# Probabilities times V: one matmul for each head in 32 array columns, and a plain copy of its output

## The reference

```python
q = (x @ Wq.T).reshape(B, N, H, d).transpose(0, 2, 1, 3)
kv = (y @ Wkv.T).reshape(B, N2, 2, H, d).transpose(2, 0, 3, 1, 4)
attn = jnp.einsum('bhnd,bhmd->bhnm', q * scale, k)
attn = jnp.where(pad_mask[:, None, :, None], attn, jnp.float32(-1000000000.0))
attn = jax.nn.softmax(attn, axis=-1)
out = jnp.einsum('bhnm,bhmd->bhnd', attn, v)
```

## Time and profile before

| what | value |
|---|---|
| median of three runs | 1987.46 us |
| the profiled execution's own time | 1987.12 us |
| its span, first to last instruction | 1985.3 us |
| granted TensorE clock, mean | 0.989 of 2.4 GHz |
| TensorE matmuls busy | 1889.8 us, 95% of the span |
| weight loads busy | 1466.3 us |
| VectorE busy | 1247.6 us |
| ScalarE busy | 1069.4 us |

### The profile page before, as it was taken

One profiled execution on the slowest core, in us unless ns is written; L12 is line 12 of the kernel. 1 busy time (PEld: TensorE's weight loads), 2 busy tenths in 40 slices (PEclk: granted clock), 3 DMA queues, 4 the chain that ended last, 5 costly groups with the idle time before them and its releaser, 6 DMA issues. The chain is left out here.

```text
span 1985.3 us, 39511 instructions
## 1 busy us (share of the span) xinstructions
PE 1889.8 (95%) x13922; PEld 1466.3 (74%) x13923; DVE 1247.6 (63%) x2287; ACT 1069.4 (54%) x1695; POOL 619.5 (31%) x641
## 2 busy tenths in 40 slices
PE   6999999999999999999999999999948999999997
PEld 6888888888888887888888888888734444444443
DVE  3555555554545555555555565555549999999995
ACT  3444444444444443434444444444318999999996
POOL 1101011010101111010101021010028999999994
PEclk9999999999999999999999999999979999999999
DMA  4111111111211111111221111111132222222221
GB/s 143 32 61 48 43 48 43 48 46 52 83 44 48 43 48 44 49 43 50 54 75 50 43 48 43 48 43 43 30 122 70 96 86 89 95 95 93 83 72 38
DMA packets 56198, 120.61 MB, mean 61 GB/s; under 512 B 5692, under 2 KB 5692, under 8 KB 56028
## 3 DMA queue, kind: packets, MB, share of 16 engines
q1 hardware_dynamic: 55828, 119.82, 18.8%
q10 hardware_dynamic: 328, 0.25, 0.0%
HBM read 101.64 MB, written 29.43 MB: 66 GB/s over the span
## 5 line engine op out<-in xcount | busy, mean ns | idle before, releaser
L417 ACT ACTIVATE prob<-psum,nmax 114x750 f32<-114x750 f32 x256 | 225.4, 885 | 251.7 <-DVE nmax L591 251.7
L338 POOL TENSOR_TENSOR y_l<-y,y_h 128x750 fp32r<-128x750 f32 x93 | 156.6, 1706 | 551.2 <-ACT y_h L403 551.2
L408 ACT ACTIVATE k_h<-psum 128x376 fp32r<-128x376 f32 (+1 forms) x256 | 124.0, 484 | 353.6 <-PE psum L846 352.2
L596 DVE TENSOR_TENSOR k_l<-psum,k_h 128x376 fp32r<-128x376 f32 (+1 forms) x256 | 139.7, 546 | 276.7 <-ACT k_h L408 276.0
L591 DVE TENSOR_REDUCE nmax<-psum 114x1 f32<-114x750 f32 x256 | 228.4, 934 | 104.2 <-PE psum L835 100.0
L846 PE MATMUL psum<-y_h,wkv_h 128*128 128x376 f32 (+1 forms) x768 | 277.1, 361 | 1.1 <-DVE q_l L584 1.1
L846 PE MATMUL psum<-y_l,wkv_h 128*128 128x376 f32 (+1 forms) x768 | 255.9, 333 | 0.0
L846 PE MATMUL psum<-y_h,wkv_l 128*128 128x376 f32 (+1 forms) x768 | 255.8, 333 | 0.0
L856 PE MATMUL psum<-wkv_h,y_h 128*125 128x512 f32 x576 | 237.6, 413 | 0.7 <-DVE wkv_l L655 0.7
L1441 PE MATMUL psum<-w_q,hq_t 128*128 128x512 bf16 x896 | 205.8, 383 | 25.4 <-ACT yo L1297 25.4
L856 PE MATMUL psum<-wkv_l,y_h 128*125 128x512 f32 x576 | 227.6, 395 | 0.0
(11 more groups left out here) (117 smaller groups left out, 3369.0 us busy)
## 6 DMA issues: line engine op xcount, KB each, us to landing
y<-in_ctx_t SPq DMA_DIRECT2D x32, 1125.0 KB, 8.0
w_part<-in_w_t SPq DMA_DIRECT2D x32, 512.0 KB, 8.1
xb<-in_x SPq DMA_DIRECT2D x56, 256.0 KB, 2.7
ab<-attn_rows SPq DMA_DIRECT2D x56, 256.0 KB, 2.9
out_rows<-yo SPq DMA_DIRECT2D x56, 256.0 KB, 2.0
attn_rows<-vmean_rows SPq DMA_DIRECT2D x32, 336.0 KB
attn_rows<-attn SPq DMA_DIRECT2D x32, 112.0 KB
xa<-in_x SPq DMA_DIRECT2D x30, 112.0 KB
```

The lines of the kernel that those rows point to most:

```text
L338: pool.tensor_tensor(y_l[:, slot, c, :], y[:, c, :], y_h[:, slot, c, :].bitcast(F32), ALU.subtract).then_inc(a_yl, 1)
L408: act.activation(k_h[:, g, s0:s1], ps_proj[k_bank[par][g, hf]][:, 0:s1 - s0], ACT.Copy).then_inc(a_kh, 1)
L417: act.activation(prob[:, e, :], ps_score[e][0:RP], ACT.Exp, bias=nmax[:, i:i + 1], accum_out=den[:, i:i + 1]).then_inc(p.exp, 1)
L596: dve.tensor_tensor(k_l[:, g, s0:s1], ps_proj[k_bank[par][g, hf]][:, 0:s1 - s0], k_h[:, g, s0:s1].bitcast(F32), ALU.subtract).then_inc(a_k ...
```

## The change

`weighted` takes each head by itself: 32 columns of V, the 57 columns of `prob_t` that belong to the head, and 32 output partitions of `ps_o`, which shrinks from [128, 4, 114] to [128, 4, 57]. So there are four matmuls for each chunk of keys where there were two, each half as wide in both directions, in four strips of 32 array columns. `heads_out` becomes one copy of 128 x 57. `head_one`, its eight memsets and the semaphore `own_o` go.

```diff
@@ set-up of tiles
-        head_col, head_one = sb("head_col", [128, 2]), sb("head_one", [128, 2])
+        head_col = sb("head_col", [128, 2])
-        ps_o = psum[:, 6, 0:NG * RP].rearrange("p (g n) -> p g n", g=NG)
+        ps_o = psum[:, 6, 0:NG * RM].rearrange("p (g n) -> p g n", g=NG)
@@ VectorE, set-up
                     for e in range(2):
                         dve.memset(head_col[HD * i:HD * i + HD, e:e + 1], SCALE if i % 2 == e else 0.0).then_inc(a_head, 1)
-                        dve.memset(head_one[HD * i:HD * i + HD, e:e + 1], 1.0 if i % 2 == e else 0.0).then_inc(a_head, 1)
-                dve.wait_ge(a_head, 4 * HPG)
+                dve.wait_ge(a_head, 2 * HPG)
@@ VectorE
                 def heads_out(p, n, g):
                     dve.wait_ge(p.o, NG * n + g + 1 + ONE)
-                    dve.tensor_scalar(o_t[:, g, :], ps_o[:, g, 0:RM], head_one[:, 0:1], 1.0, ALU.mult, ALU.mult).then_inc(own_o, 1)
-                    dve.wait_ge(own_o, 1)
-                    dve.scalar_tensor_tensor(out=o_t[:, g, :], in0=ps_o[:, g, RM:RP], scalar=head_one[:, 1:2], in1=o_t[:, g, :],
-                                             op0=ALU.mult, op1=ALU.add).then_inc(p.oe, 1)
-                    dve.sem_clear(own_o)
+                    dve.tensor_copy(o_t[:, g, :], ps_o[:, g, :]).then_inc(p.oe, 1)
@@ TensorE, weighted
                     for j in range(MJ):
-                        for e in range(2):
-                            w = 128 * g + PW * e
-                            mm = pe.matmul(ps_o[PW * e:PW * e + PW, g, :], v[:, slot, j, w:w + PW], prob_t[:, g % 2, e, j, :],
+                        for h in range(HPG):
+                            w = 128 * g + HD * h
+                            mm = pe.matmul(ps_o[HD * h:HD * h + HD, g, :], v[:, slot, j, w:w + HD],
+                                           prob_t[:, g % 2, h // 2, j, RM * (h % 2):RM * (h % 2) + RM],
                                            start=(j == 0), stop=(j == MJ - 1))
```

More of the change, by code:

```diff
@@ L160, in gated_cross_attention_bit_ffn @@
         a_fill = sem("a_fill")
-        own_ident, own_var, own_dve, own_w, own_o = sem("own_ident"), sem("own_var"), sem("own_dve"), sem("own_w"), sem("own_o")
+        own_ident, own_var, own_dve, own_w = sem("own_ident"), sem("own_var"), sem("own_dve"), sem("own_w")
         met_pe, met_pool, met_sp, met_slow = sem("met_pe"), sem("met_pool"), sem("met_sp"), sem("met_slow")
@@ L386, in _ @@
                 act.activation(gates[:], gates_in[:], ACT.Tanh).then_inc(a_gate, 1)
-                act.wait_ge(a_head, 4 * HPG)
+                act.wait_ge(a_head, 2 * HPG)
                 def turned(p, n):
```

## The result

The changed kernel takes 1959.2 us as the median of four runs (1954.35 to 1960.81), against 1987.33 us for the kernel before in the same runs (1986.92 to 1988.34). The ratio is 0.9854, with a 95% interval of 0.9835 to 0.9872. It is faster by 28 us where 68 were forecast, and it lies outside the range. Its profiled execution took 1954.35 us.

The account below looks back on a forecast made before the run. The prediction took TensorE's in-order work to bound stage A. From 1987.12 us it took 70.0 for blocks, added 1.5 handed back and subtracted 0.3 for the copy: 1918.3, or 1918.7 as median, called 1919; range 1908 to 1945.

Parts of the forecast that it names:

- first part: Stage A: TensorE's own work in order, busy 1357.21 of 1373.00 us, so savings show whole unless VectorE is late.
- The block, 0.76 us: One `weighted` on TensorE: 12 rounds of 47.5 ns plus 0.18 and 0.01 us, down from 1.32, saving 0.56.
- the fixed rest: In each `weighted` block: 0.18 us for getting in and draining, beside the 12 rounds; possibly as low as 0.12.
- (b): `weighted`: only two strips at a time, or a 24 ns start floor; block stays 1.32 us, total 1987; chance 0.07.
- (c): `weighted`: two strips, each half held to 59 ns by weight load; block 1.60 us, total 2022; chance 0.07 shared with another.
- rival (a): `weighted`: four strips together, but something other than streaming sets the round, 59 ns or somewhat above; total 1935; chance 0.14.
- The rule of 60 cycles: `weighted` matmuls: some 60 cycles of overhead each make a round 50 ns, not 47.5; 4 us more, 1923.
- floor of 24 ns: `weighted`: any matmul start costs 24 ns whatever its strip, so 48 starts take 1.15 us and nothing changes.
- 125 of 128 blocks: Stage A: all `weighted` blocks save 0.56 us except groups 0 to 2 of the last batch; 70.0 us.
- The copy, 206 ns: `heads_out` on VectorE: 206 ns in place of 548, 44 us in all, nearly all hidden; 0.34 us shows.
- The time handed back, 1.5 us: `scores` of group 3 in seven late even batches: 0.22 us each lost to longer waits for VectorE.
- The sum, 1918.7: Whole kernel: 1987.12 us less 68.8 gives 1918.3, plus 0.34 for the median of the runs.

Follow-up runs that it names:

- e7_copy_alone: Kernel before with only VectorE's plain copy of the first 57 columns, TensorE unchanged, heads in the other columns left out: 1996.0 us, ratio 1.0042.
- e3_split_columns: Kernel before, still two strips of 64, with each matmul of `weighted` split into two of 57 columns: 2073.28 us.

## Why the prediction was wrong, and where it was right

The step that failed is in its first part: "any time that one piece gives back is given back by the whole, except where VectorE is the one that is late". It counted the 3072 matmuls and as many loads that the change adds as time in the array alone. They are also 384 rows more in a round of a loop of two batches, and these took the body past the length up to which the jump back is short: 13 jumps of 3.3 to 3.9 us in place of 0.21, with 25.9 us of waits in the array and more time at the lower clock behind them. The diff of the change shows the doubled matmuls plainly; the question that was not asked is where a round of the loop gets its instructions from. None of the rivals had this mechanism either.

In the profiled execution the account is: 1987.1, less 72.5 for the blocks; plus 25.9 for 13 waits at the jumps (21.3 + 4.6); plus 2.3 for longer waits for `prob_t`; plus the half-clock stretches. For `v_chunk` these are 13.2 us: the busy time of its three groups rose from 237.6 + 227.6 + 227.6 to 242.2 + 232.5 + 231.3. The clock gives the same from the other side: 37.5 - 10.2 = 27.3 us more at half speed, and half of that is 13.7. Together 1956.0, where 1954.35 was measured. Whether a wait ends in a half-clock stretch varies, and the changed kernel's four runs lie 6.5 us apart where those of the kernel before lie 1.4 apart.

Point by point:

- *The block, 0.76 us.* Right: 0.74. Four strips run side by side at 50 ns a round, close to the forecast 47.5, and the fixed rest is 0.74 - 0.60 = 0.14 us, not 0.18. The prediction's 95 ns for the kernel before is a mean that takes in one short first step; behind it the rounds start 98 ns apart in the trace, and with these the rest is 0.14 there too. The two errors nearly cancel. Rivals (b) and (c) are out, and so are the 59 ns of rival (a).
- *The rule of 60 cycles.* The 60 cycles for each pass (the Trainium skill, TensorEngine Tiling (Array Packing), Instruction Overhead) would make a round 50 ns by the prediction's estimate. That is what the rounds take. But with 114 columns, too, they take 3 ns more than the prediction's two clocks a column (98 against 95), so the runs do not tell that rule from the stream. A floor of 24 ns between any two starts is ruled out by the four records that begin within 30 ns.
- *125 of 128 blocks.* Right: in the last batch `turn_prob` waits 1.25 to 1.28 us for the exponential behind the blocks of groups 0 to 2, against 0.68 in the earlier trace rows, so what these blocks gain is lost there.
- *The copy, 206 ns.* Right: 209 ns on average, and hidden.
- *The time handed back, 1.5 us.* About right in size (2.3), by luck. The prediction had the early batches keep pace and the late ones lose 0.22 us each. In fact the late waits grew by 0.1 (1.62 to 1.73) and the early ones, from 0.57 to 0.81 from `turn_out` to `scores`, by 0.24. The term left out that GpSimd holds VectorE up: in the early batches L575 (L574 after the change) took 0.36 us in place of 0.18. That VectorE's own work sets the late waits is borne out by e7_copy_alone; why they grew by half of the forecast is open.
- *The sum, 1918.7.* It is the time of the changed kernel with its jump mended: 1918.25. That the two agree this closely is in part luck: the blocks gave 72.5 us and not 70.0, and more than 1.5 was handed back.

## What to carry to other kernels

Count the instructions that a change adds to a hardware loop, not only their time on the engine: here a saving of 68 us lost 40 at 13 jumps, and three quarters of the same change lost nearly all of its gain. A short stall once a round, put down to an innocent semaphore, with more packets on the queue of the program, is its mark; a prefetch hint or a loop written out took it away here. And an engine that gets faster can hit a neighbour at a worse moment: look at what a suspiciously long small operation ends together with.

## What was not expected of the hardware

- TensorE's jump back took 0.21 us with 1458 and 1650 rows of the trace in the body and 3.3 to 3.9 us with 1746 and 1842; about 2 us of this reach the array. A straight program read 119 packets of 16 KB, nearly as many, and its time was that of the hinted kernel (1919.01 and 1918.25 us).
- With the hint a body of 1843 rows jumped back in 0.22 us and was not read again at all.
- A wait of 2 us at the full clock was followed by a stretch at 1.2 GHz in 10 of 13 cases in the changed kernel and in all 13 with six of eight groups changed. In the former this cost some 13 us on top of 25.9.
- VectorE's product of two columns in SBUF (L575) ends with GpSimd's subtraction: 0.15 us alone, up to 1.75 in e3_split_columns. The pass over 512 columns behind it takes 0.55 us alone and 2.0 beside GpSimd. VectorE's copies out of PSUM beside the same GpSimd work kept their 0.69 us.
- Rounds of records of 57 columns start 58 ns apart in two strips of 64 weights, and 50 ns apart in four strips of 32.
